# Normalising half of the tiles on VectorE instead of ScalarE in a windowed attention block

## What is computed

```
h   = layernorm(win) * g1 + b1                # over the 96 channels
q, k, v = h @ wq + bq, h @ wk + bk, h @ wv + bv   # 3 heads of 32
attn = softmax(q k^T / sqrt(32))              # inside a window of 64 tokens
win = win + (attn v) @ wo + bo
h2  = layernorm(win) * g2 + b2
win = win + gelu(h2 @ w1 + b1m) @ w2 + b2m    # 96 -> 384 -> 96
```

## Time and profile before

| | us |
|---|---|
| median of 3 runs (5439.17 to 5441.29) | 5439.2 |
| the profiled execution, own time | 5443.8 |
| its span in the profile | 5442.0 |

### The profile page before, as it was taken

One profiled execution on the slowest core, in us unless ns is written; L12 is line 12 of the kernel. 1 busy time (PEld: TensorE's weight loads), 2 busy tenths in 40 slices (PEclk: granted clock), 3 DMA queues, 4 the chain that ended last, 5 costly groups with the idle time before them and its releaser, 6 DMA issues.

```text
span 5442.0 us, 275140 instructions
## 1 busy us (share of the span) xinstructions
PE 5176.5 (95%) x105172; PEld 4395.4 (81%) x105172; DVE 4179.8 (77%) x9862; ACT 3741.6 (69%) x7758; POOL 3083.7 (57%) x3053
## 2 busy tenths in 40 slices
PE   6999999999999999999999999999999999999999
PEld 4887888878788787888878888788887888878888
DVE  6968768687686877869778697786977869688696
ACT  6839568495784957749477594875938659396693
POOL 5645646466464655646556466464664646556464
PEclk8999999999999999999999999999999999999999
DMA  3011020110201102010120201202011020110201
GB/s 98 3 44 48 27 68 6 47 42 27 68 9 51 36 30 65 11 57 27 33 62 15 61 19 36 59 16 66 13 38 57 19 70 6 41 54 22 73 3 44
DMA packets 92300, 213.96 MB, mean 39 GB/s; under 512 B 22058, under 2 KB 26379, under 8 KB 91851
## 3 DMA queue, kind: packets, MB, share of 16 engines
q1 hardware_dynamic: 91848, 208.20, 13.0%
q10 hardware_dynamic: 2, 0.00, 0.0%
HBM read 107.45 MB, written 100.66 MB: 38 GB/s over the span
## 4 chain that ended last, share of the span: by engine, by line
PE 88%; issue 5%; DVE 5%; SPq 1%; ACT 1%; POOL 0%; DVEq 0%; ACTq 0%; DMA 0%; POOLq 0%
PE psum L585 20%; PE psum L599 19%; PE psum L462 12%; PE psum L430 8%; PE psum L508 6%; PE psum L477 6%; PE psum L494 6%; PE psum L538 5%; PE psum L524 5%; DVE row_max L828 1%; DVE stats L807 1%; DVE stream L857 1%; SPq L251 1%; DVE probs L835 0%; DVE prob_sum L843 0%
## 5 line engine op out<-in xcount | busy, mean ns | idle before, releaser
L297 POOL TENSOR_TENSOR probs<-probs,prob_inv 128x512 f32<-128x512 f32 x771 | 783.1, 1044 | 1496.7 <-DVE prob_inv L851 1496.6
L857 DVE TENSOR_TENSOR stream<-stream,psum 128x384 f32 x1024 | 562.4, 553 | 850.3 <-PE psum L599 760.8
L736 ACT ACTIVATE gelu_odd<-psum 128x512 f32<-128x512 f32 x768 | 459.9, 599 | 732.7 <-PE psum L585 676.9
L736 ACT ACTIVATE gelu_even<-psum 128x512 f32<-128x512 f32 x768 | 459.6, 598 | 682.8 <-PE psum L585 627.1
L376 POOL TENSOR_TENSOR stream<-stream,b_all 128x768 f32 x256 | 493.2, 1931 | 612.4 <-DVE normed L877 584.8
L659 ACT ACTIVATE normed<-stream,shift,rstd 128x96 f32 (+1 forms) x2072 | 770.7, 461 | 43.9 <-POOL shift L345 23.2
L807 DVE BATCH_NORM_STATS2 stats<-stream (+2 forms) x4224 | 725.9, 243 | 57.1 <-DVE stream L857 38.9
L336 POOL TENSOR_TENSOR rstd<-variance,minus_half 128x32 f32<-128x32 f32 (+3 forms) x181 | 747.7, 4131 | 14.2
L304 POOL TENSOR_TENSOR hT<-hT_upper,hT_lower 96x1024 f32<-96x1024 f32 x258 | 613.6, 2378 | 22.8 <-issue 15.6
L828 DVE TENSOR_REDUCE row_max<-psum 128x8 f32<-128x512 f32 x771 | 523.8, 679 | 131.7 <-PE psum L494 116.6
L843 DVE TENSOR_REDUCE prob_sum<-probs 128x8 f32<-128x512 f32 x771 | 497.8, 679 | 109.1 <-ACT probs L693 109.1
(11 more groups left out here) (86 smaller groups left out, 10635.3 us busy)
## 6 DMA issues: line engine op xcount, KB each, us to landing
stream<-in_x SPq DMA_DIRECT2D x272, 192.0 KB
out<-stream SPq DMA_DIRECT2D x256, 192.0 KB
stream<-in_x SPq DMA_DIRECT2D x272, 180.0 KB
out<-stream SPq DMA_DIRECT2D x256, 180.0 KB
stream<-in_x SPq DMA_DIRECT2D x544, 6.0 KB
out<-stream SPq DMA_DIRECT2D x512, 6.0 KB
gelu_odd<-in_L_conv_w SPq DMA_DIRECT2D x1, 144.0 KB
w_w<-in_L_conv_w SPq DMA_DIRECT2D x1, 144.0 KB
```

Source lines behind the costliest of these rows:

```text
L297: nc.gpsimd.tensor_tensor(block_h, block_h, inv, ALU.mult).then_inc(probs_ready, 1)
L736: nc.scalar.activation(gelu[parity][:, j, part * SHARES:(part + 1) * SHARES], psum[:, UP_BANKS[part][j], :], ACT.Gelu).then_inc(gelu_done, 1)
L857: nc.vector.tensor_tensor(part, part, psum[:, banks[g], 0:GROUP], ALU.add).then_inc(added, 1)
```

## The change

Tiles 0 to 3 of `normalise1` go to DVE, as two TENSOR_TENSOR operations over 128 x 384 elements, a product with `rstd1` and a sum with `shift1`, both read with a stride of zero over the 96 channels of a tile. They stand at the head of DVE's attention step, before `maxima`. The first waits for `rstd1_ready` and for the first half of the last unit's transposes (`t1_done` at 2u - 1), the second for the first (`scale1_step`). ACT keeps tiles 4 to 7 with its waits as they were. `ln1_ready`, one semaphore counted twice per unit, becomes one semaphore for each half.

```
-        ln1_ready = sem("ln1_ready")
+        scale1_step = sem("scale1_step")
+        ln1_ready = [sem("ln1_ready_first"), sem("ln1_ready_second")]
...
             def transpose1(u, g):
-                pe.wait_ge(ln1_ready, 2 * u + g + 1)
+                pe.wait_ge(ln1_ready[g], u + 1)
...
-            def normalise1(u, index, g):
-
-                if g == 0:
-                    wait_apart(act, rstd1_ready, u + 1)
-                    if not (isinstance(u, int) and u == 0):
-                        wait_apart(act, t1_done, 2 * u)
+            def normalise1_second(u, index):
+
+                wait_apart(act, rstd1_ready, u + 1)
+                if not (isinstance(u, int) and u == 0):
+                    wait_apart(act, t1_done, 2 * u)
                 slot = u % SLOTS if isinstance(u, int) else u & (SLOTS - 1)
-                for t in range(g * (TILES // 2), (g + 1) * (TILES // 2)):
+                for t in range(TILES // 2, TILES):
                     last = nc.scalar.activation(normed1[:, t, :], stream[:, slot, t * C:(t + 1) * C], ACT.Identity,
                                                 bias=shift1[:, index, t:t + 1], scale=rstd1[:, index, t:t + 1])
-                last.then_inc(ln1_ready, 1)
+                last.then_inc(ln1_ready[1], 1)
...
                 back, middle, front = u, u + 1, u + 2
-                for g in range(2):
-                    normalise1(u + 3, index, g)
+                normalise1_second(u + 3, index)
...
+            def normalise1_first(u):
+
+                index = u % BATCH if isinstance(u, int) else u & (BATCH - 1)
+                tiles = slice(0, TILES // 2)
+
+                def per_tile(stat):
+                    return stat[:, index, tiles].unsqueeze(2).to_broadcast((P, TILES // 2, C))
+
+                wait_apart(dve, rstd1_ready, u + 1)
+                if not (isinstance(u, int) and u == 0):
+                    wait_apart(dve, t1_done, 2 * u - 1)
+                nc.vector.tensor_tensor(normed1[:, tiles, :],
+                                        stream[:, slot_of(u), 0:GROUP].rearrange("p (t c) -> p t c", c=C),
+                                        per_tile(rstd1), ALU.mult).then_inc(scale1_step, 1)
+                dve.wait_ge(scale1_step, u + 1)
+                nc.vector.tensor_tensor(normed1[:, tiles, :], normed1[:, tiles, :], per_tile(shift1), ALU.add)\
+                    .then_inc(ln1_ready[0], 1)
+
             def attention_step(u, half):
 
                 back, middle = u, u + 1
+                normalise1_first(u + 3)
```

## The result

The changed kernel takes 5823.8 us (median of 4 runs, 5822.5 to 5825.3), the kernel before beside it 5439.2: ratio 1.071, 95% interval 1.069 to 1.073, or 385 us more. The forecast was 5787 with a range of 5500 to 5860.

What follows compares the result with a forecast made beforehand. PE, ACT and DVE were nearly full; DVE, blocked by `unite_hT`, would set the pace. Per batch 20.2 + 0.2 + 1.4 = 21.8, times 16 = 348 us, giving 5792 profiled, 5787 median; range 5500 to 5860.

Steps and rivals of the forecast that it cites:

- The place of the loss: DVE's attention step: first new operation shut out until POOL's `unite_hT` ends, finishing 0.42 us after it; chance 0.68.
- Who stands: DVE and POOL operations meeting in SBUF: whoever came second stands until the first is done; the wait is not shared.
- The cycle: DVE's attention step, first row maximum to the next: 12.54 us, setting the pace where steps took 10.985.
- The distance to PE: From DVE's first row maximum to PE's next scores: fixed at 7.73 us when the maximum is late.
- Steps 3 to 14: These attention steps of a batch: each takes 12.54 us, +1.555, with +1.36 once in step 7.
- step 2: Third attention step of a batch: begins on time, first maximum about 3.6 us behind the scores, +0.2 us.
- step 7: Eighth attention step of a batch: POOL's 1.48 us normalisation slips between the two new DVE operations, +1.36 us once.
- the entry into the MLP stage: End of a batch's attention: step 15's +1.555 us delay is passed on through `add_attention` and `copy_h2T`.
- The head of the pair: Two waits and address registers ahead of DVE's pair: 0.22 us, hidden in the 12.54 us cycle.
- first rival: No exclusion at `unite_hT`: DVE's cycle 10.91 us in plain steps, 12.50 with extra statistics; 5503 us; chance 0.15.
- ACT's relief: ACT's attention step loses 1.44 us, freeing PE's 0.31 us idle per step: 64 us, 5375; rival's chance 0.03.
- Clock: PE's granted clock may fall; PE's 1.9 us standing per step absorbs it first; up to 5860 us; chance beyond that 0.03.

Runs made afterwards that it cites:

- (2): The changed kernel with one more wait: POOL starts `unite_hT` only when the next unit's pair is done, pair still at the head; 5584.1 us, ratio 1.026.
- (8): The changed kernel with `unite_hT`'s sum left out, POOL filling the tile twice with constants, writing without reading; 5598.9 us, ratio 1.029.
- experiment 3: The changed kernel without DVE's pair except for the first unit; DVE keeps its waits, ACT normalises only tiles 4 to 7; 5381.6 us, ratio 0.989.
- (4): The kernel before, all eight tiles on ACT, with the pair added at DVE's head, writing to a buffer nobody reads; 5831.1 us, ratio 1.071.
- (7): The changed kernel with the pair between DVE's second shift and third maximum instead of at the head; 5543.8 us, ratio 1.018.

## Why the prediction was right

**The place of the loss.** DVE sets the pace, shut out by `unite_hT`. Shown from three sides: the product ends 0.41 to 0.42 us behind `unite_hT` wherever it starts (forecast 0.42); moving `unite_hT` away brings the loss from 385 to 138 us (2); leaving its reads out brings it to 157 (8). Step 10 is the exception: there the product ends mostly 0.79 us behind `unite_hT`, because two of POOL's short statistics operations stand in between (0.42 behind the second of them).

**Who stands.** The prediction read that whoever came second stood. By the recorded starts that does not hold: in (8) DVE's sum starts at 1197.17, before POOL's operation at 1197.40, and in all 16 batches it is the sum that stands, to 0.42 us behind POOL's end. The forecast did not hang on it, since `unite_hT` starts before the product in every step that counts.

**The cycle.** Forecast 12.54 us per step. Measured from one first maximum to the next: 1308.82 less 1296.20 = 12.62, and in looped steps 1181.15 less 1168.49 = 12.66. The starting rows in DVE's timeline:

```profile
1168.49 0.68 DVE L827 TENSOR_REDUCE row_max<-psum 128x8 f32<-128x512 f32 x1
...
1296.20 0.68 DVE L827 TENSOR_REDUCE row_max<-psum 128x8 f32<-128x512 f32 x1
```

In the looped steps the extra 0.1 lies in the pair: from the product's end (1180.55) to the sum's start (1180.67) 0.12 us, not the 0.03 that was taken from a maximum and its shift. In the step of 12.62 that gap is 0.04, and the sum is long, 0.62.

**The distance to PE.** Forecast 7.73 us from the first maximum to PE's next scores. In step 10 these rows of DVE's and PE's timelines give 1291.36 less 1283.61 = 7.75:

```profile
1283.61 0.68 DVE L827 TENSOR_REDUCE row_max<-psum 128x8 f32<-128x512 f32 x1
```

```profile
1291.36 1.28 PE L495 MATMUL psum<-kT,qT 32*64 32x64 f32 x96 [0.26 <-issue]
```

**The sizes that were off.** The whole is 385 us where 348 were forecast, 24.0 per batch instead of 21.8. Steps 3 to 14 give 152.76 less 131.82 = 20.9, where 12 x 1.555 + 1.36 = 20.0 were forecast. The term that was most off is step 2, priced at 0.2 us: in the fourth batch it takes 12.66 (1176.23 to 1188.89) where it took 11.19 (1106.47 to 1117.66), so 1.5; in the mean of all batches 12.4 against 11.1, so 1.3. The reason for 0.2 was that `unite_hT` is held up by PE in step 1 and over before the pair comes. That was read from the fourth batch alone. Its step 1 took 15.0 us, while that of the others took 10.9 to 13.6, and over the whole run before `unite_hT` waited for PE only this once (us, times):

```profile
PE psum L477: 1.4, 1
```

After, `unite_hT` ran there at 1177.74 in its usual place and the pair met it, as the rows above show. The premise was one batch's accident.

In step 7 POOL's normalisation did get in between the two new operations, as forecast, and cost 1.06 us instead of 1.36 (the step takes 13.72, the one before it 12.66). Timeline of DVE, then of POOL:

```profile
1242.14 1.71 DVE L909 TENSOR_TENSOR normed<-stream,rstd 128x384 f32 x1 [0.48 <-issue]
1243.98 1.62 DVE L913 TENSOR_TENSOR normed<-normed,shift 128x384 f32<-128x384 f32 x1
```

```profile
1243.40 1.78 POOL L366 TENSOR_TENSOR normed<-stream,mean 128x768 f32<-128x768 f32 x1
```

The rest went the other way and adds up: step 2 is 1.1 us over its forecast, steps 3 to 14 are 0.9 over, step 7 included, and the entry into the MLP stage 0.2 (from the scores of step 15 to those of the next batch it is 1.7 us longer, where 1.555 were forecast). That is the 2.2 us per batch by which the forecast was low.

**The head of the pair.** Forecast 0.22 us, hidden. It is hidden in the changed kernel, but where it is bare it is 0.48 us, and 0.87 at a turn of the loop. The first rival's time came out low for that reason: 5503 forecast for no exclusion, 5584 and 5599 measured with the exclusion taken away (2, 8). It had 10.91 us for plain steps; in (2) DVE's cycle is 11.5 and 11.9 in looped steps and 10.73 in the last ones.

**ACT's relief.** Its bound, 64 us, was what experiment 3 measured, and under DVE's pace it is worth nothing (4).

**Clock.** The granted clock in the stretch is 0.98 where it was 1.00, and PE's busy time 132.68 against 128.14 us. With PE standing 20 of 152.76 us, that was absorbed, as the prediction said. Steps 13 and 14, by window:

```profile
1316.56:1329.09 12.53, 12.26 (x288) 10.39 (x289) 12.21 (x26) 9.83 (x22) 5.36 (x5) 0.86 0.00 0
1329.09:1341.65 12.56, 10.77 (x289) 8.87 (x289) 12.24 (x26) 9.61 (x22) 5.38 (x5) 1.00 0.00 0
```

At a granted clock of 0.86 PE is busy 12.26 us instead of 10.77, and the step is no longer. Nine of the run's steps 2 to 14 were at 0.86 to 0.88, each as long as its like at full clock.

## What to carry to other kernels

Before giving work to an engine, look at what its neighbour runs at that moment: here a DVE operation that reads two tensors from SBUF cost its own time only where POOL was idle, only wrote or computed its power, and beside POOL's sums and products of large tiles the rest of POOL's operation too. The price hangs on the place in the order more than on the amount: half of the tiles kept 78% of the loss, another place in the same step took away 73% of it (5544 against 5824).

Busy shares did say where relief was worth something, but the relief has to go to an engine that is waiting at that point: POOL stood 5.9 us per step and took the same pair at a gain.

## What the runs showed of the hardware that was not expected

Ahead of the pair, whose waits are the same in every step, DVE stood 0.48 us in looped code, 0.87 at the loop's turn, and next to nothing in most unrolled steps (1304.58 + 1.38 against 1305.87; 0.21 in step 10). That the waits and address registers are what takes this time is inferred: the trace shows only that nothing else did.

A POOL operation gets in between two DVE operations that depend on each other, as in step 7 above, where the sum took 1.62 us instead of 0.56; in (8) it took 2.11 although by the records it had started first. In the other order short POOL operations of 0.2 us were stretched to 0.5, as beside this pair:

```profile
1307.79 0.53 POOL L318 TENSOR_TENSOR mean_gap<-stats 128x8 f32<-128x8 f32 x1
1308.28 0.20 POOL L319 TENSOR_TENSOR spread<-stats 128x8 f32<-128x8 f32 x1
1308.45 0.53 POOL L320 TENSOR_TENSOR mean_sum<-stats 128x8 f32<-128x8 f32 x1
```

POOL's power operation leaves DVE alone even near its start. In (7), in each of the 16 batches, the product comes up 0.23 to 0.28 us behind it and takes its 0.55 (POOL, then DVE):

```profile
1224.03 2.91 POOL L337 TENSOR_TENSOR rstd<-variance,minus_half 128x16 f32<-128x16 f32 x1
```

```profile
1224.30 0.55 DVE L909 TENSOR_TENSOR normed<-stream,rstd 128x384 f32<-128x384 f32 x1
```

So what shuts DVE out is not that a two-input POOL operation is running. It may be the time in which it still reads, which would be short for 16 elements per partition; no run here shows the reads themselves.
